# Local convolution of a five-part network: two columns taken together, whole-array products first, quarter-array products after

## What is computed

```python
vimg = vh.transpose(0, 2, 1, 3).reshape(b, H, W, c).transpose(0, 3, 1, 2)
lepe = lax.conv_general_dilated(vimg, lepe_w, (1, 1), 'SAME', feature_group_count=c)
lepe = lepe + lepe_b[None, :, None, None]
```

## Time and profile before

| what | value |
|---|---|
| median of 3 runs | 3067.09 us (3066.92 to 3069.07) |
| the profiled execution, own time | 3078.55 us |
| its span | 3076.7 us |
| mean granted TensorE clock | 0.945 |
| busy share of the span: TensorE, VectorE, ScalarE, GpSimd | 88%, 70%, 44%, 10% |
| local convolution, both passes | 1398.24 to 1555.83 us |
| whole-array products (L1034) | 256 instructions, 90.9 us busy |
| quarter-array products (L1035, L1036) | 256 instructions each, 81.4 us busy each |

### The profile page before, as it was taken

The page is one execution under the profiler, slowest core; times in us unless marked ns, Lnnn a source line. Parts: engine busy times, 40 slices in busy tenths (PEclk is TensorE's granted clock), DMA queues, the critical chain, the costliest instruction groups (busy, mean ns, idle before and its releaser), DMA issues. The chain is left out here.

```text
span 3076.7 us, 71764 instructions
## 1 busy us (share of the span) xinstructions
PE 2698.7 (88%) x25712; PEld 2429.3 (79%) x25712; DVE 2166.5 (70%) x5168; ACT 1361.2 (44%) x2113; POOL 298.9 (10%) x816
## 2 busy tenths in 40 slices
PE   5888879999999999928978888886999999999791
PEld 4666669999999999923457676666999999999791
DVE  7888856776667677767028887886766767677865
ACT  2777642246642222236445565652225663222120
POOL 1112110000000011135000100010000000000602
PEclk9998989999999999958989999998999999999695
DMA  4333320000000000079247888777000000000759
GB/s 91 83 83 87 91 113 0 0 0 0 0 0 0 0 0 0 0 222 230 48 42 88 108 101 101 98 91 120 0 0 0 0 0 0 0 0 0 124 94 130
DMA packets 735623, 164.91 MB, mean 54 GB/s; under 512 B 728208, under 2 KB 728848, under 8 KB 730640
## 3 DMA queue, kind: packets, MB, share of 16 engines
q1 hardware_dynamic: 608640, 132.08, 24.8%
q10 hardware_dynamic: 126864, 31.19, 6.2%
HBM read 96.13 MB, written 67.11 MB: 53 GB/s over the span
## 5 line engine op out<-in xcount | busy, mean ns | idle before, releaser
L271 PE MATMUL L_conv<-L_x_hi,L_w_hi 128*128 128x248 f32 (+2 forms) x5040 | 1218.1, 279 | 51.1 <-DVE L_w_lo L234 29.1
L271 PE MATMUL L_conv<-L_x_hi,L_w_lo 128*128 128x248 f32 (+2 forms) x5040 | 1209.7, 279 | 0.0
L158 ACT ACTIVATE L_row_b<-S,L_bias 128x256 f32 (+1 forms) x1008 | 513.4, 510 | 1120.2 <-DVE L_x_hi L212 1109.8
L271 PEld LDWEIGHTS L_conv<-L_x_hi,L_w_hi 128*128 128x128 f32 x5040 | 959.1, 190 | 55.3 <-issue 29.2
L271 PEld LDWEIGHTS L_conv<-L_x_hi,L_w_lo 128*128 128x128 f32 x5040 | 960.6, 191 | 0.0
L222 DVE SCALAR_TENSOR_TENSOR S<-L_conv,L_neg_bias,L_row_b 128x256 f32 x1008 | 487.3, 483 | 446.1 <-PE L_conv L276 445.8
L276 PE MATMUL L_conv<-L_x_lo,L_w_hi 128*128 128x248 f32 (+2 forms) x5040 | 750.8, 279 | 6.6 <-DVE L_x_lo L214 6.6
L276 PEld LDWEIGHTS L_conv<-L_x_lo,L_w_hi 128*128 128x128 f32 x5040 | 659.5, 191 | 10.3 <-DVE L_x_lo L214 9.9
L214 DVE TENSOR_TENSOR L_x_lo<-S,L_x_hi 128x256 fp32r<-128x256 f32 x1016 | 466.5, 459 | 34.7
L212 DVE TENSOR_SCALAR L_x_hi<-S 128x256 fp32r (+1 forms) x1016 | 320.8, 316 | 41.4 <-PEq L47 6.2
L607 PE MATMUL dc_conv<-dc_xz_hi,dc_w_hi 128*128 128x512 f32 x384 | 170.8, 445 | 6.5 <-DVE dc_w_lo L734 6.5
(11 more groups left out here) (202 smaller groups left out, 2829.1 us busy)
## 6 DMA issues: line engine op xcount, KB each, us to landing
dc_raw<-x SPq DMA_DIRECT2D x32, 512.0 KB, 6.6
x_scratch<-dc_raw SPq DMA_DIRECT2D x16, 1024.0 KB, 7.5
at_res<-x_scratch SPq DMA_DIRECT2D x32, 512.0 KB, 11.7
x_scratch<-at_res SPq DMA_DIRECT2D x64, 256.0 KB, 5.8
fs_buf<-x_scratch SPq DMA_DIRECT2D x32, 512.0 KB, 6.7
sh_G<-x_scratch ACTq DMA_DIRECT2D x56, 256.0 KB, 6.0
out<-fs_buf SPq DMA_DIRECT2D x32, 256.0 KB, 4.4
out<-fs_buf ACTq DMA_DIRECT2D x32, 256.0 KB, 4.8
```

What stands on the lines that cost most here:

```text
L158: nc.scalar.activation(row_b[p][:, :, :], line(k, at_step(k, i), p), ACT.Identity, bias=bias[:, k:k + 1]).then_inc(row_b_ready[p], 1)
L271: nc.tensor.matmul(out[:, to, :], w[:, k, s * P:(s + 1) * P], x_hi[p][:, at, :], start=(s == PADJ and n == 0), stop=False)
```

## The change

TensorE's columns are taken in pairs: the whole-array product of w, that of w + 1, then the two quarter-array products of w, and those of w + 1. The waits for banks stay with the whole-array products, and `taps_done` with the last quarter product of each column. The group products that stood ahead of a column now stand ahead of its pair, so those of odd columns (7, 21, 35, 49) come one column earlier. The programs of the other engines are the same.

```diff
@@ -1026,29 +1026,41 @@
                 pe.wait_ge(me_ready, n + 1)
                 nc.tensor.matmul(group_ps[:, 2 * n:2 * n + 2], avg[:, :], me, start=True, stop=True).then_inc(group_done, 1)
 
-            def taps_of(p, w):
+            def bank_of(p, w):
+                return taps[(p * W + w) % 4][:, 0:J * NB].rearrange("p (i b) -> p i b", b=NB)
+
+            def whole_tile(p, w):
                 g = p * W + w
                 if g >= 4:
                     pe.wait_ge(taps_kept, g - 3)
-                out = taps[g % 4][:, 0:J * NB].rearrange("p (i b) -> p i b", b=NB)
-                nc.tensor.matmul(out, bands.band0[:, w, :], column(every, slice(0, J), w, p), start=True, stop=False)
+                nc.tensor.matmul(bank_of(p, w), bands.band0[:, w, :], column(every, slice(0, J), w, p), start=True, stop=False)
+
+            def quarter_tiles(p, w):
+                out = bank_of(p, w)
                 nc.tensor.matmul(out[lo, 1:J, :], bands.band1[hi, w, :], column(hi, slice(0, J - 1), w, p), start=False, stop=True)
                 nc.tensor.matmul(out[hi, 0:J - 1, :], bands.band1[lo, w, :], column(lo, slice(1, J), w, p),
                                  start=False, stop=True).then_inc(taps_done, 1)
+
+            def two_columns(p, w):
+                whole_tile(p, w)
+                whole_tile(p, w + 1)
+                quarter_tiles(p, w)
+                quarter_tiles(p, w + 1)
 
             pe.wait_ge(consts_in, 2 * 16)
             for n in range(NB + 1):
                 group(n)
             pe.wait_ge(normed, NB)
-            for w in range(W):
+            for w in range(0, W, 2):
                 if w % 16 == 0:
                     pe.wait_ge(bands.loaded[w // 16], 2 * 16)
-                if w and w % GROUP_EVERY == 0 and w // GROUP_EVERY < NB:
-                    group(NB + w // GROUP_EVERY)
-                taps_of(0, w)
+                for c in (w, w + 1):
+                    if c and c % GROUP_EVERY == 0 and c // GROUP_EVERY < NB:
+                        group(NB + c // GROUP_EVERY)
+                two_columns(0, w)
             pe.wait_ge(normed, B)
-            for w in range(W):
-                taps_of(1, w)
+            for w in range(0, W, 2):
+                two_columns(1, w)
 
         @block.vector
         def _(dve):
```

## The result

The change made the kernel faster: 3058.93 us median of 8 runs against 3070.64 of 8 runs of the kernel before, ratio 0.9959, 95% interval 0.9943 to 0.9976, which is 12.6 us less (7.4 to 17.5). The forecast was 13.6 us less. A second measurement gave 0.9965 (0.9952 to 0.9977), 10.8 us less.

What follows compares the result with a forecast made beforehand. TensorE's own pace was taken to bound the stage. Gains of 11.0 us in the second pass and 2.6 in the first (11.0 less 8.4 of waits) made 13.6 off 3067.09: 3053.5 us, range 3046 to 3062.

Steps and rivals of the forecast that it cites:

- The switch: Both passes: half the whole-to-quarter array changes saves 0.345 us a pair, 2.045 instead of 2.39, 11.0 us a pass.
- The rivals with exposed weights (3061 and 3069): Pairs: second column's first weight load exposed, 3061 us, chance 0.10; every weight load exposed, 3069.3 us, chance 0.07.
- The bank waits: First pass: TensorE waits for PSUM banks behind ScalarE's normalises, 1.73 us behind even columns, 0.32 to 0.54 behind odd, 8.4 together.
- 2.6 were forecast: First pass: 11.0 us saved on switches less 8.4 us of waits for banks, a gain of 2.6 us.
- The group products: First pass: those for odd columns go one column earlier, VectorE still keeps up, cost nothing.
- VectorE's wait turned uneven: First-pass sign: VectorE's wait for the group product goes from 0.55 us to nearly nothing or turns uneven.
- all-or-nothing rival: First pass: clock at 0.5 from column 13 to the end, 46 us lost, 3091 us, chance 0.05.
- a 0.5 in the clock row inside a pass: Sign in the profile after: a granted clock of 0.5 inside a pass would show the prediction wrong.
- The row that the prediction gave for a fall: Ahead of this stage: clock at 0.50 after 10 us of idling, cited in favour of a clock fall.
- The rival of VectorE's loop: First pass without bank waits: VectorE's sample loop binds, 18.1 us gained in all, 3049.0 us, chance 0.10.
- part 4: First-pass group products: VectorE's loop, 8.04 us of its own, would be the next limit if the bank waits were gone.
- a margin of 0.26 us: First pass before the change: four columns last 4.78 us against ScalarE's 4.52 around a normalise, leaving 0.26 us.

Runs made afterwards that it cites:

- seven banks: Seven PSUM banks for the columns instead of four: on the changed kernel ratio 0.9936, first pass 69.53 us; on the kernel before, as control, 1.0002.
- each pass alone: Changed kernel with one pass put back to single columns: ratio 0.9966 with pairs in the second pass, 1.0000 with pairs in the first.
- pairs in the first pass only: Changed kernel with the second pass put back to single columns: ratio 1.0000, first pass 79.73 us.
- fours: Changed kernel with four columns grouped instead of two, and seven PSUM banks: 3043.44 us median, ratio 0.9902.
- the second pass alone: Changed kernel with the first pass put back to single columns: ratio 0.9966, second pass 67.25 us.
- the normalise moved: Changed kernel, four banks, ScalarE's normalise one column later where it stood behind the first of a pair: ratio 0.9944, first pass 72.38 us.
- the kernel with eight waits of 1.1 to 1.3 us: Kernel before with each column's two quarter-array products replaced by one whole-array product: one run, first pass 70.20 us, second 56.51.
- waits of 1.9 to 2.1 us at eight places: Changed kernel with three PSUM banks instead of four: ratio 1.0015, first pass 100.09 us.

## Why the prediction was right

**Right, step by step.** The size of the gain (13.6 forecast, 12.6 and 10.8 measured, 13.35 in the first profile's stretch). The time itself, 3053.5, was 5.4 us under the measured 3058.93, and 3.55 of that is the base: the forecast was set against 3067.09, the median of three runs, and the eight runs beside the changed kernel have 3070.64. *The switch*: a pair at 2.045 us (measured 2.05), 11.0 us for the second pass (11.05), all later weight loads hidden. The rivals with exposed weights (3061 and 3069) fell with the first lines of the timeline, and with them, as far as this case goes, the rule that the prediction quotes from Part 3 of the Trainium skill's page "TensorE: Matmul & The Clock Gate" ("What overlaps and what doesn't"): whole-array loads ran ahead under whole-array products of the same rows, 0.21 us apart. *The bank waits*: 1.73 us counted, 1.76 seen, 0.32 counted and seen behind odd columns; 8.4 us together, 8.7 when seven banks took them away (8.4 without the difference in the half clock at the start). That the first pass gains 2.3 of its 11 us, 2.5 without that difference, where 2.6 were forecast, is shown by four runs that each change one thing: banks, place of the normalise, each pass alone. *The group products*: they cost nothing, and VectorE's wait turned uneven.

**Mis-sized: the clock.** The prediction held the clock at full speed in its sum and had its fall as an all-or-nothing rival with 46 us of loss, chance 0.05; and it named a 0.5 in the clock row inside a pass as a sign of being wrong. The first profile doesn't have it, the two later ones of the changed kernel do. It comes in pieces: the four profiles with four banks and the long waits (the changed kernel three times, pairs in the first pass only once) had none, one, one and two stretches of some 3.4 us at 0.5 in the first pass, which then took 78.23, 79.29, 79.73 and 81.47 us, 1.45 us more on the mean than the first. That belongs in the term "8.4 us of waits", which is about 10 us. That is enough to bring 13.6 down to 12.1, between the two measurements; the intervals are too wide to prove that by the run times. In six profiles without those waits (before, with seven banks with and without pairs, fours, the second pass alone, the normalise moved) there was no such stretch inside either pass behind the half clock at the start, and none in the kernel with eight waits of 1.1 to 1.3 us. That the waits bring it on rests on this count of profiles; what exactly makes the clock fall at one wait and not at the next wasn't settled. The row that the prediction gave for a fall doesn't show one: the 0.50 at the start of the stage had been there for 76 us (since 1321.8), so it did not come from the 10 us of idling.

**The rival of VectorE's loop** ("six intervals win 0.55 each") was wrong as a cap, and so was part 4 where it calls this loop the next limit. Both took the pace of one engine for the end of the pass. The loop began the pass with a lead over the engine that depends on it (ScalarE), and with only four intervals of 8 us behind sample 9 the pass was too short to use that lead up.

## What to carry to other kernels

Where products on the whole array and on parts of it alternate, group those of one size: here each round trip cost 0.345 us, as much as 40% of a column's streaming, and the profile shows it only as "issue" idle time of the weight loader with TensorE "100% busy". Before regrouping, count the buffers at the moment when the consumer is away longest: a group that needs two free banks at once turns a margin of 0.26 us into waits of 1.7 us, and waits can cost the clock on top. More banks gave the whole gain. Moving the consumer's long job to the end of a group gave about two thirds of what the waits had taken (5.85 of 8.7 us) without another bank. With seven banks, larger groups then gave more.

## What the hardware showed that I had not expected

Idle times of 1.5 us in a stream that is otherwise full were sometimes followed by a stretch at 1.2 GHz of about 3.4 us, beginning 0.7 to 2 us after TensorE had resumed and while it was fully busy; with waits of 1.9 to 2.1 us at eight places 30 of 95 us ran so, beginning 0.1 to 0.6 us after TensorE had resumed. The Trainium skill ("TensorE: Matmul & The Clock Gate", "A second HAM failure mode: psum-queue depth-cycling") describes a swing of that kind in a kernel that goes round PSUM banks; here a stretch at half clock came behind 4 of 16 waits of about 1.5 us (the long ones in four profiles) and behind 6 of 8 of about 2 us. I had set it aside since the kernel before showed none, but its ring had no stalls in it.
